# Extra transposes of the identity ahead of the state transposes, in a Mamba and mixture-of-experts layer on one core

## What is computed

```python
def step(h, inp):
    d_t, B_t, C_t, x_t = inp
    dA = jnp.exp(d_t[..., None] * A)
    h = h * dA + d_t[..., None] * B_t[:, None, :] * x_t[..., None]
    y_t = jnp.sum(h * C_t[:, None, :], axis=-1)
    return (h, y_t)
...
x = _layernorm(x + mamba(x))
x = _layernorm(x + experts(x))
```

## Time and profile before

| | |
|---|---|
| median of 3 runs | 2401.52 us |
| profiled execution, time | 2402.95 us |
| profiled execution, span | 2401.1 us |
| mean granted TensorE clock | 0.907 |
| TensorE (PE) busy | 2088.5 us, 87% |
| VectorE (DVE) busy | 2080.6 us, 87% |
| GpSimd (POOL) busy | 1817.9 us, 76% |
| ScalarE (ACT) busy | 1516.3 us, 63% |
| state transposes (L885), 4096 | 592.1 us busy |
| `y` (L1290), 512 | 646.0 us busy |
| scans (L1432), 1024 | 1200.4 us busy |

### The profile page before, as it was taken

How to read it: one execution, slowest core, us unless ns; L and a number is a source line. 1 busy time by engine, 2 the same in 40 slices (tenths; PEclk the granted TensorE clock), 3 DMA queues, 4 the chain that set the end, 5 groups by cost and what they waited for, 6 DMA issues and landing times.

```text
span 2401.1 us, 29781 instructions
## 1 busy us (share of the span) xinstructions
PE 2088.5 (87%) x8544; PEld 1217.3 (51%) x8544; DVE 2080.6 (87%) x2284; ACT 1516.3 (63%) x2586; POOL 1817.9 (76%) x1460
## 2 busy tenths in 40 slices
PE   7886879898989989899889989899898989888874
PEld 2444555555545555545545555545555555554532
DVE  3799999999999899998999989989999889999400
ACT  3747755785577766677577765768566775545322
POOL 1859997788887888779887888869887788776212
PEclk9897789898998999999899999989998899779887
DMA  3412031357544574356743674436752475477394
GB/s 99 145 53 84 19 125 60 114 176 256 155 111 145 198 263 123 106 165 216 269 110 116 210 265 130 128 137 207 257 133 91 156 244 180 127 233 235 76 378 120
DMA packets 210752, 385.08 MB, mean 160 GB/s; under 512 B 29048, under 2 KB 29304, under 8 KB 210592
## 3 DMA queue, kind: packets, MB, share of 16 engines
q1 hardware_dynamic: 196256, 349.63, 43.5%
q0 software_dynamic: 14336, 33.56, 6.7%
HBM read 297.15 MB, written 85.98 MB: 160 GB/s over the span
## 4 chain that ended last, share of the span: by engine, by line
DVE 27%; PE 22%; POOL 18%; issue 11%; ACT 4%; DMA 3%; SPq 1%; DVEq 0%; POOLq 0%; ACTq 0%
DVE hst L1432 14%; PE bank L873 13%; POOL dbu L1268 11%; DVE y L1290 7%; PE hTp L885 5%; DVE u L1318 2%; POOL u L1256 2%; POOL delta L1253 2%; PE bank L991 1%; DMA zs<-sorted_tokens 1%; ACT tokT L1143 1%; ACT dA L1180 1%; PE hTp L919 1%; DVE st L1296 1%; POOL sorted_tokens L1204 1%
## 5 line engine op out<-in xcount | busy, mean ns | idle before, releaser
L1268 POOL TENSOR_TENSOR dbu<-u,Bbc 128x512 f32<-128x512 f32 x1024 | 1308.1, 1313 | 298.0 <-DVE hst L1432 293.1
L1432 DVE TENSOR_TENSOR_SCAN hst<-dA,dbu 128x512 f32<-128x512 f32 x1024 | 1200.4, 1205 | 29.1 <-ACT dA L1180 25.9
L1180 ACT ACTIVATE dA<-delta,negA 128x512 f32<-128x512 f32 x1024 | 701.9, 689 | 477.8 <-DVE hst L1432 475.9
L885 PE MATMUL hTp<-ident,hst 128*128 128x128 f32 x4096 | 592.1, 298 | 124.5 <-DVE y L1290 43.9
L885 PEld LDWEIGHTS hTp<-ident,hst 128*128 128x128 f32 x4096 | 515.8, 154 | 363.9 <-DVE y L1290 143.9
L1290 DVE SCALAR_TENSOR_TENSOR y<-hTp,Ct,y 128x1024 f32<-128x1024 f32 x512 | 646.0, 1262 | 41.8 <-PE hTp L885 38.4
L873 PE MATMUL bank<-wslot,hidT 128*128 128x512 f32 x512 | 241.7, 607 | 16.7 <-ACT zs L1132 13.0
L873 PE MATMUL bank<-delta,tokT 128*128 128x512 f32 x536 | 248.3, 600 | 4.1 <-issue 2.2
L873 PE MATMUL bank<-wslot,tokT 128*128 128x512 f32 x496 | 236.5, 607 | 6.6 <-ACT tokT L1143 4.7
L873 PE MATMUL bank<-hidT,wslot 128*128 128x512 f32 x384 | 190.2, 639 | 12.8 <-DVE u L1318 9.7
L1318 DVE SCALAR_TENSOR_TENSOR u<-bank,cw,u 128x511 f32<-128x511 f32 (+2 forms) x192 | 142.3, 743 | 32.9 <-ACT u L1065 28.0
(11 more groups left out here) (131 smaller groups left out, 2238.8 us busy)
## 6 DMA issues: line engine op xcount, KB each, us to landing
wslot<-in_w_expT SPq DMA_DIRECT2D x86, 1024.0 KB
Bbc<-b_scratch SPq DMA_DIRECT2D x128, 256.0 KB
sorted_results<-ysb SPq DMA_DIRECT2D x113, 256.0 KB, 5.8
zs<-sorted_tokens SPq DMA_DIRECT2D x105, 256.0 KB, 4.0
wslot<-in_w_inT SPq DMA_DIRECT2D x26, 1024.0 KB
res<-in_w_expT SPq DMA_DIRECT2D x18, 1024.0 KB, 5.7
gate_scratch<-zs SPq DMA_DIRECT2D x64, 256.0 KB, 2.0
spare<-gate_scratch SPq DMA_DIRECT2D x56, 256.0 KB, 5.2
```

What stands on the lines that cost most here:

```text
L885: mm = nc.tensor.transpose(hTp[i % 2][:, tok(j)], hst[n % 2][:, j, tok(i)], ident[:, :])
L1180: nc.scalar.activation(dA[j % 2][:, :], delta[w.odd][:, j, :], ACT.Exp, scale=negA[:, j, n:n + 1]).then_inc(exp_done, 1)
L1268: nc.gpsimd.tensor_tensor(dbu[j % 4][:, :], u[w.odd][:, j, :], Bbc[n % 2][:, :], ALU.mult).then_inc(dbu_done, 1)
L1432: nc.vector.tensor_tensor_scan(hst[n % 2][:, j, :], dA[j % 2][:, :], dbu[j % 4][:, :], 0.0, ALU.mult, ALU.add).then_inc(scan_done, 1)
```

## The change

Each timetable gets a list `fill`: for every second step, the count of *extra* transposes, from the shares that stand behind that state part. A 512-column matmul counts 8, a side transpose piece 4, the small matmuls of router and `Ct` nothing, and the part's own eight transposes count 8. What is missing to 14 is made up with transposes of the identity matrix. They are written to the columns of `hTp[i % 2]` that the part's own transposes overwrite right behind them, so nothing reads them. They stand behind the waits for `acc_done` and `turned_taken`. The wait for `scan_done` of the first part moves from the front to behind them. The last four parts of the kernel get none.

```diff
+COLUMNS = {"yT": 4, "x1T": 4, "xsT": 4, "xsL": 4, "yinit": 4, "dt": 2, "wT": 8, "yTF": 4, "x1TF": 4, "wTF": 4, "gateT": 32, "bias": 4, "Ct": 0, "count": 0, "gate": 0, "logits": 0, "logF": 0}
+ENOUGH = 14
...
+        done = [ND + sum(COLUMNS.get(x[0], 8) for row in (k, k + 1) for x, _ in self.rows["pe"][row]) for k in range(0, steps, 2)]
+        self.fill = {2 * k: max(0, ENOUGH - n) for k, n in enumerate(done)}
...
-            def state_part(G, n, i, first, turns):
-
-                if i == 0:
-                    pe.wait_ge(scan_done, G * ND + ND)
+            def state_part(G, n, i, first, turns, fill):
+
                 if not (first and n == 0 and i < 2):
                     pe.wait_ge(acc_done, G * NH + (i - 1))
                 if not (isinstance(turns, int) and turns == 0):
                     pe.wait_ge(turned_taken, turns)
+                for j in range(fill):
+                    nc.tensor.transpose(hTp[i % 2][:, tok(j % ND)], ident[:, :], ident[:, :])
+                if i == 0:
+                    pe.wait_ge(scan_done, (G + 1) * ND)
                 for j in range(ND):
                     mm = nc.tensor.transpose(hTp[i % 2][:, tok(j)], hst[n % 2][:, j, tok(i)], ident[:, :])
                 mm.then_inc(hT_done, 1)
...
-                        state_part(w.b * NS + (n - 1), (n - 1) % NS, j // 2, first, w.turned_base + w.seg.turned_by[step])
+                        state_part(w.b * NS + (n - 1), (n - 1) % NS, j // 2, first, w.turned_base + w.seg.turned_by[step], w.seg.fill[step])
...
-                    state_part(NB * NS - 1, NS - 1, i, False, w.turned_base)
+                    state_part(NB * NS - 1, NS - 1, i, False, w.turned_base, 0)
```

## The result

The changed kernel takes 2433.99 us (median of 4 runs, 2424.13 to 2434.34), the kernel before 2400.96 us (median of 4). The ratio is 1.0107, with a 95% interval of 1.0078 to 1.0136: it is slower by 19 to 33 us. The forecast was 2430 us in a range of 2408 to 2450. The profiled execution has a span of 2432.5 us, 31.4 more than before.

A forecast was written before the change was run, and what follows sets the result against it. VectorE (DVE) was taken as the bound, held up by TensorE where `y` waits for state transposes. Exposed parts 30.7, carry-over 3, clock credit minus 5 gave +28.7 us on 2401.5: 2430 us, range 2408 to 2450.

The forecast's parts named there:

- the 36 parts: Parts given six extras whose `y` already waited 0.25 us or more for state transposes: together 22.7 us longer.
- The sum of 30.7 us: Cost of all 50 parts where extras delay DVE: 22.7 us, 3.8 us and 4.2 us; bounds nothing to 100 us.
- The three half-clock parts: One part each in three SEG_FULL periods, behind slow bias matmuls, ending as DVE asks: 3 x 1.28 = 3.8 us.
- the eleven short ones: Eleven parts ending 0.02 to 0.50 us before DVE asks: 7.1 us, of which slack leaves 4.2 us.
- Carry-over: Where TensorE runs without a gap, hidden extras push back the next exposed part: 3 us, from 0 to 8.
- The clock's credit: Time regained from a higher clock, a third of 14.8 us in SEG_FULL: minus 5 us, bounds 0 and minus 21.
- the bias and `Ct` stretch: Bias matmuls and `Ct` in each SEG_FULL period: low clock loses 14.8 us there over the five periods.
- The SEG_PRO stretch: Stretch of SEG_PRO with only state parts: its clock would be near 1.0 and its time the same.
- Faster by the clock: Bias and `Ct` work of SEG_FULL: the clock stays up and drains the backlog, 2381 to 2394 us; chance 0.06.
- No cost: Extras run while TensorE waits anyway and change nothing: 2401 us, within 7 us; chance 0.06.
- TensorE the bound everywhere: Every filled part of SEG_TWO and the five SEG_FULL is exposed: 2473 us, from 2450 up; chance 0.08.
- No answer of the clock: Whole kernel: transposes do not count as busy, extras leave the clock as it is: 2435 us; chance 0.10.

The follow-up runs named there:

- the other extras only: 580 extras at the 100 filled parts where TensorE was not late, none at the 59 late ones, against the kernel before: 2401.13 us, ratio 0.9992.
- the first four experiments: In the text's order, against the kernel before: wait order alone 0.9976; extras at late parts only 1.0112; at the others only 0.9992; half the extras everywhere 0.9999.

## Why the prediction was right

- **The place decides.** Right, and the main point: 354 extras at 59 late parts carry the loss, 580 at 100 others carry none on balance. In the change the 59 parts have 61.2 us of `y` waits where they had 30.9, which is all of the growth.
- **The price.** Right: 0.64 us for each exposed part at full clock. Among the 36 parts where DVE already waited, 20 grew by 0.60 to 0.70 us in the trace of the change.
- **The sum of 30.7 us.** It came out close, partly by terms that cancel. By the waits of `y` in the two traces, the 36 parts gave 16.2 us for the 22.7 of the sum. Five of them have less wait than before (0.83, 1.21, 0.96, 0.86 and 1.07 us became 0.21 three times and 0 twice). The sum took each exposed part by itself, with the wait that one trace shows for it. But with the other extras only, none of them at these five, the waits are 0, 1.23, 1.23, 0 and 0: they differ between kernels whether extras stand there or not, and the extras can't be given the credit for their going. The three half-clock parts gave 2.5 for 3.8 (two paid 1.3 each and one nothing), the eleven short ones 5.8 for 4.2.
- **Carry-over, 3 us from 0 to 8.** Parts outside the three lists gave 5.6 us of `y` waits, in the range and above the estimate. Delayed side pieces had no term: `u` waits 4.0 us more. The 9.2 us more for the logits are made up behind them.
- **The clock's credit, 5 us.** About right, but it can't be read off by itself. In the bias and `Ct` stretch four of the periods now have 0.91 and one 0.94, where they had 0.84 to 0.97. In windows of 54 us DVE's work is the same, 245.4 us in all five before and with the change: the worst periods gained (47.4 to 49.2) and the best lost (52.0 to 49.2). From `y` to `y`, the same work took 305.0 us where it took 301.5. The `y` waits in it grew by 11.8 us, from 6.9 to 18.7, and the other waits fell by 8.0, from 16.4 to 8.4. The forecast's credit of 5 us has these 8.0 us to answer to. A share of them may be DVE's coming later; but with the other extras only, where `y` waits as before, the other waits fell by 7.5 us too.
- **What it said the trace would show.** `y` waits of about 65 us: 68.7. A mean clock of 0.93 or more: 0.928. The SEG_PRO stretch near 1.0 at the same time: 0.88, and DVE busy 41.00 of 41.00 us. DVE's busy time unchanged at 2080: 2073.4, by the `gap` and `pick` of the router. The tail behind the last `y`: 166.8 us before and 166.0. The wait of 0.95 us would become 1.6: it became 1.90, since extras of the part before add to it; the one of 1.60 us became 2.12 to 2.26, not 1.9, so TensorE's idle time ahead of it did not absorb what was expected.
- **The rivals.** Faster by the clock: out, the clock rose by 0.021 and the time by 1.1%. No cost: out. TensorE the bound everywhere, 2473 us: not reached by transposes; the plain matmuls, twice the work, reach 2481. No answer of the clock: out, by the stretch in SEG_PRO, though the measured 2434 us lies next to its 2435: the time alone would not have told the two apart. Against the first rival the prediction counts seven waits for filled parts between 1303 and 1425 us. There are seven waits, five of them at filled parts; in the other periods it is four or five, so the argument stands.
- **Where it was luck.** Of the terms, 33.7 us of exposed parts and carry-over came out as 30.3 and the credit of 5 as 8.0. That gives 22 us, and the span grew by 31.4. The 9 us between are items that had no term, `u` with 4.0 the largest that was found. So a part of the closeness of 2430 to 2434 is luck.

## What to carry to other kernels

Filler work on an engine costs its own length wherever another engine already waits for it, and next to nothing where that engine has more time to spare than the filler takes; twice the filler may no longer fit. So choose its places by the idle time ahead of them in a trace, not by how little work a timetable puts behind them. A timetable leaves a row empty both where there is nothing to do and where the engine is late, and a rule that reads the row can't tell these apart. A higher mean clock is no gain by itself: look for the one stretch in which the bound engine waits on TensorE at low clock, and put the filler ahead of that. And before you count a longer wait as a cost, add up everything from the wait to the next instruction of the main chain: a wait can grow while what stands behind it shrinks.

## What the runs showed of the hardware

- An fp32 matmul of 128 columns was issued as two instructions (1868 for 934), an fp32 transpose as one (934 for 934), and the plain one cost nearly three times as much in the kernel's time: a ratio of 1.0312 against 1.0107.
- A busy TensorE did not hold the full clock by being busy. In the stretch of 205 to 246 us, TensorE busy 41.00 of 41.00 us with many 8-row matmuls had 0.54; busy 31.07 us with 128-row ones, 1.00.
- The same kernel's time goes with its mean clock. Of 29 runs of the kernel before beside the first four experiments, one with a mean clock of 0.902 took 2419 us and one with 0.912 took 2398, and over all the correlation is -0.81. Which low-clock stretches make the difference was not looked at run by run. Between kernels it does not hold: 0.927 came with 2401 us, 0.911 with 2399.
- Small DVE instructions took six to eight times as long beside GpSimd's: a cast of 128x8 took 1.30 us and ended with the GpSimd instruction that ran beside it, and 0.17 us between two of GpSimd's.
